# A prologue of an adaptive-norm block on one Trainium2 core: the decay table's round trip put ahead of the bulk loads, and weight checks, casts, a residual, statistics and two flag operations moved

## The chip, the cores and the metric

The kernel runs on one core of one Trainium2 chip (trn2). The metric is the device time of one execution in microseconds (us). The engines are TensorE (PE), VectorE (DVE), ScalarE (ACT), GpSimd (POOL) and SyncE (SP); SP and ACT issue DMAs, and each of the two has one DMA queue in this program.

## The reference

One transformer-like block on x of 4 x 2048 x 256 (float32). A modulation of six rows per batch comes from `silu(c) @ wmod`. With it:

```python
ga = sign(ga) * max(|ga|, 0.25)           # gb likewise
h = layernorm(x) * (1 + ca) + sa
x = x + ga * attn(h)
h = layernorm(x) * (1 + cb) + sb
x = x + gb * ffn(h)
```

`attn` is a linear-attention memory with 4 heads of 64: tokens go in chunks of 64, keys are the normalised `h` of the token before, and each head has a decay `gamma = sigmoid(decay)`. In a chunk the products of keys are weighted by `gamma ** (i - j)`; a unit triangular matrix of 64 x 64 is inverted; then a state of 64 x 64 for each batch and head passes from chunk to chunk. `ffn` has two gated input layers (256 to 1024, silu), two layers 1024 to 1024 with gelu and one back to 256; its weights are -1, 0 or 1 with one scale for each output.

## The kernel before

The 2048 tokens are 32 steps of 64 (`STEPS`). In every step the attention of the step and the dense layers (`l1`, `l2`, `l3`, `y`) of the one before are interleaved on PE. The order on every engine is written out by hand: lists of items such as `("gram", 0)` are walked by each engine's `part()`, which does its own share of that item. `alone` is the list of the first step's attention, with no dense layers to run beside it; `opening` follows it, and ends where the first dense layer (`l1` of the list `second`) can start; then come `second`, `third` and the loop over `mixed`. The engines meet only through semaphores, and each engine works through its items strictly in its list's order, so an item that waits holds back all behind it on that engine. SP and ACT also keep their DMA issues in program order.

What the prologue has to do, and the names:

- **Decay table.** GpSimd computes `powers` (gamma to the distance, L698) from `decay` and the first part of the constants. The table is written to DRAM (`pow_dram`, the DMA `decay_powers<-powers`, semaphore `pow_out`) and read back twice in a shifted form (`hank<-decay_powers`, `pow_in`). PE spreads it (`tables`, L1283), and DVE makes the masks of it (`level_mask` L1047, `intra_mask`). Without them no `near`, `cross` or `far` (products of keys under a mask, on POOL, L617) can be made, so no inverse. DVE copies the turned keys to `rT` behind `level_mask`.
- **Inverse.** `fs` on DVE gives 8 x 8 inverses, `expand` makes `inv`; then `n` 1, 2 and 3 on PE and DVE, then the copies `diag` on ACT (L716), then `solve` (own values and corners).
- **Bulk loads.** SP loads the second part of the modulation weights (`wmod_sb`, 1024 KB), then the dense weights into `w_raw`: 22 loads of 512 KB, two to a unit, 11 units (0 to 10). Unit i is issued only when unit i-3 has landed (`hi_in`). Among them stand the tokens of step 1 (`y<-in_x`) and the key rows of step 0 (`kg<-r`, `last<-r`).
- **Checks.** The item `check` on ACT reads the low halves of a unit of weights (L731, 11 in all, `checked`), to see that they are zero. DVE reduces the result (`flag` 0, L1071, waits for all 11), PE turns it, DVE makes `flag_i` of it (`flag` 1), and PE and SP branch on it; on the given weights the branch to the exact rounded weights is taken.
- **Casts.** The item `round` copies units into `w_hi` (four on POOL, L628, the rest on ACT and POOL later). PE's first `l1` waits for those four, for `intra_ready` and for `xl_ready`.
- **Gates.** `cols` multiplies `wmod_sb` on PE (L1265) and makes the small gate columns on DVE (`gate_done` counts to 5); `spread` and `gates` widen them.
- **Residual and statistics.** `residual` on POOL is `base` = x + h * ga in two operations (L643, L645); `stats` are the layer norm's sums of step 1 on DVE (L838), `length` the reciprocal norm `rinv` on POOL (L605), `unit` the normalised keys `r` on DVE (L878).
- **End of the prologue.** `attn_out` gives x1 of step 0, `norm2` its normalised form `xn` (DVE L1007), `turn` and `ln2` (ACT, eight operations) `h2`, `parts` its two halves `xh` and `xl`, `sweep` 1 and `intra` belong to step 1's attention. `warm` items are matmuls on PE whose result nobody reads (L1158).

## Time and profile before

| | |
|---|---|
| median of 3 runs | 1749.15 us (1746.56 to 1749.63) |
| the profiled execution | 1747.17 us, its span 1745.3 us |
| mean granted TensorE clock | 0.993 |
| PE busy | 1714.9 us, 98% of the span |
| DVE, ACT, POOL busy | 64%, 55%, 34% |
| first dense matmul (L1169) | 68.16 us after the span's start |
| DMA traffic by fortieths of the span | 327 GB/s in the first (43.6 us), 3 to 31 GB/s in every later one |

The table is read from the page: its part 1 gives the busy times, part 2 the granted clock by slices, part 3 the queues. The span is the trace's own length; the time beside it also holds what lies around the span, 1.87 us here. Times of steps below are counted from the span's start.

### The profile page before, as it was taken

How to read it: one execution, taken by the hardware profiler on the slowest of the kernel's cores; microseconds unless marked ns; L12 is line 12 of the kernel's file. 1: busy time of each engine (PE TensorE's matmuls, PEld its weight loads, DVE VectorE, ACT ScalarE, POOL GpSimd, SP SyncE). 2: the span in 40 equal slices, each digit the busy share in tenths (PEclk: the TensorE clock that was granted, in tenths of full speed). 3: DMA queues.
4: the chain of work that ended last, by engine and by line, in shares of the span. 5: the costliest groups of instructions: out<-in, count | busy, mean ns of one | idle time of the engine just before them, and what ended most of it. 6: DMA issues, size and time to landing. Idle time of an engine off the chain costs nothing.

```text
span 1745.3 us, 60527 instructions
## 1 busy us (share of the span) xinstructions
PE 1714.9 (98%) x25489; PEld 1650.2 (95%) x25489; DVE 1115.6 (64%) x3038; ACT 964.3 (55%) x2251; POOL 592.9 (34%) x694
## 2 busy tenths in 40 slices
PE   7799999999999999999999999999999999999999
PEld 4698999999999999999999999999999999999998
DVE  4778666666666666666666676666666666666432
ACT  4664555555555555555555555555555555555554
POOL 3544332342332343333243333243233233343111
PEclk8999999999999999999999999999999999999999
DMA  9001000000000000000000000000000000000000
GB/s 327 31 14 29 15 23 23 15 23 11 24 23 24 18 20 11 24 23 24 18 20 14 22 23 23 18 19 20 15 23 23 22 16 19 16 23 17 8 3 12
DMA packets 37108, 47.08 MB, mean 27 GB/s; under 512 B 8864, under 2 KB 29088, under 8 KB 36832
## 3 DMA queue, kind: packets, MB, share of 16 engines
q1 hardware_dynamic: 35360, 41.80, 8.6%
q8 instruction: 206, 3.38, 0.8%
q10 hardware_dynamic: 1472, 1.34, 0.3%
q14 instruction: 70, 0.57, 0.1%
HBM read 22.53 MB, written 8.39 MB: 18 GB/s over the span
## 4 chain that ended last, share of the span: by engine, by line
PE 94%; DVE 1%; POOL 1%; issue 1%; DMA 1%; ACT 1%; ACTq 0%; SPq 0%; POOLq 0%; DVEq 0%
PE mlp L1169 64%; PE mlp L1241 6%; PE solo L1169 3%; PE solo L1316 3%; PE duo L1445 3%; PE solo L1142 2%; PE duo L1135 1%; PE duo L1366 1%; PE duo L1130 1%; PE duo L1434 1%; PE solo L1454 1%; PE duo L1339 1%; PE solo L1152 1%; PE duo L1330 1%; PE duo L1436 1%
## 5 line engine op out<-in xcount | busy, mean ns | idle before, releaser
L1169 PE MATMUL mlp<-act_hi,w_hi 128*128 128x256 f32 x4096 | 969.5, 283 | 1.2 <-POOL act_lo L664 0.5
L1169 PE MATMUL mlp<-act_lo,w_hi 128*128 128x256 f32 x4096 | 946.8, 278 | 0.0
L1169 PEld LDWEIGHTS mlp<-act_hi,w_hi 128*128 128x128 f32 x4096 | 771.1, 188 | 10.0 <-POOL act_lo L664 1.2
L1169 PEld LDWEIGHTS mlp<-act_lo,w_hi 128*128 128x128 f32 x4096 | 771.9, 188 | 1.0 <-issue 0.2
L806 ACT ACTIVATE full<-mlp,scale_sb 128x256 f32<-128x256 f32 x512 | 246.4, 481 | 558.5 <-PE mlp L1169 558.3
L897 DVE TENSOR_TENSOR act_lo<-full,act_hi 128x256 fp32r<-128x256 f32 x512 | 240.4, 470 | 318.5 <-ACT act_hi L807 315.9
L664 POOL TENSOR_TENSOR act_lo<-full,act_hi 128x256 fp32r<-128x256 f32 x256 | 186.6, 736 | 497.8 <-ACT act_hi L796 497.5
L807 ACT ACTIVATE act_hi<-mlp,scale_sb 128x256 fp32r<-128x256 f32 x512 | 242.6, 474 | 0.0
L1169 PE MATMUL mlp<-xh,w_hi 128*128 128x256 f32 x768 | 189.1, 284 | 4.8 <-issue 2.3
L1169 PE MATMUL mlp<-xl,w_hi 128*128 128x256 f32 x768 | 188.2, 281 | 0.0
L605 POOL TENSOR_TENSOR rstd<-ve,minus_half 128x2 f32<-128x2 f32 x64 | 49.0, 766 | 338.5 <-DVE ve L846 338.3
L1021 DVE SCALAR_TENSOR_TENSOR full<-mlp,scale_sb,gate 128x256 f32<-128x256 f32 x192 | 92.9, 484 | 98.1 <-ACT gate L791 93.0
L791 ACT ACTIVATE gate<-mlp,scale_sb 128x256 f32<-128x256 f32 x192 | 90.9, 474 | 109.5 <-PE mlp L1169 109.4
L1169 PEld LDWEIGHTS mlp<-xh,w_hi 128*128 128x128 f32 x768 | 144.2, 188 | 6.1 <-issue 4.6
L1169 PEld LDWEIGHTS mlp<-xl,w_hi 128*128 128x128 f32 x768 | 144.9, 189 | 0.0
L1241 PE MATMUL mlp<-w_hi,act_hi 128*128 128x256 f32 x512 | 118.2, 277 | 0.0
L1241 PE MATMUL mlp<-w_hi,act_lo 128*128 128x256 f32 x512 | 118.1, 277 | 0.0
L605 POOL TENSOR_TENSOR rinv<-ssm,minus_half 128x8 f32<-128x8 f32 x32 | 52.7, 1647 | 184.4 <-DVE ssm L875 184.4
L796 ACT CAST act_hi<-full 128x256 fp32r<-128x256 f32 x256 | 101.7, 397 | 11.3 <-DVE full L1021 11.3
L1241 PEld LDWEIGHTS mlp<-w_hi,act_hi 128*128 128x128 f32 x512 | 96.1, 188 | 0.1
L1241 PEld LDWEIGHTS mlp<-w_hi,act_lo 128*128 128x128 f32 x512 | 96.2, 188 | 0.0
L780 ACT ACTIVATE h<-solo,sbm,cb 128x64 f32<-128x64 f32 x256 | 84.0, 437 | 2.0 <-PE solo L1454 2.0
(177 smaller groups left out, 2677.4 us busy)
## 6 DMA issues: line engine op xcount, KB each, us to landing
w_raw<-in_wts SPq DMA_DIRECT2D x22, 512.0 KB, 8.4
kg<-r SPq DMA_DIRECT2D x64, 126.0 KB
xin<-in_x SPq DMA_DIRECT2D x62, 128.0 KB
out_y<-y SPq DMA_DIRECT2D x62, 128.0 KB, 2.5
step_and_inv<-square_t SPq DMA_DIRECT2D x56, 64.0 KB, 2.0
wmod_sb<-in_wmod SPq DMA_DIRECT2D x1, 1024.0 KB, 8.2
kg<-last SPq DMA_DIRECT2D x64, 2.0 KB
last<-r SPq DMA_DIRECT2D x64, 2.0 KB, 1.8
```

Source lines behind the costliest of these rows:

```text
L605: pool.tensor_tensor(dst[:], src[:], minus_half[:, 0:src.shape[1]], ALU.pow).then_inc(done, 1)
L664: pool.tensor_tensor(act_lo[0][:, k, :], full[k % 3][:], act_hi[0][:, k, :].bitcast(F32), ALU.subtract).then_inc(l_ready[0], 1)
L780: ins = act.activation(h2[:].rearrange("p k b n -> p (k b n)")[:, cols], solo[1][:, cols], ACT.Identity, bias=sbm[:, k, b:b + 1], scale=cb ...
L791: act.activation(gate[k % 2][:], gated[k % 3][:, 0:TOK], ACT.Silu, scale=scale_sb[:, 0, k:k + 1]).then_inc(l_act[0], 1)
L796: act.copy(act_hi[0][:, j, :], full[j % 3][:]).then_inc(l1_hi, 1)
L806: act.activation(full[k % 2][:], mlp[k % 2][:, 0:TOK], ACT.Gelu, scale=s)
L807: act.activation(act_hi[layer % 2][:, k, :], mlp[k % 2][:, 0:TOK], ACT.Gelu, scale=s).then_inc(l_act[layer], 1)
L897: dve.tensor_tensor(act_lo[layer % 2][:, k, :], full[k % 2][:], act_hi[layer % 2][:, k, :].bitcast(F32), ALU.subtract).then_inc(l_ready[la ...
L1021: dve.scalar_tensor_tensor(full[k % 3][:], up, s, gate[k % 2][:], ALU.mult, ALU.mult).then_inc(prod_ready, 1)
L1169: mm = pe.matmul(dst, *general_ops, start=is_first and i == 0, stop=is_last and i == 1)
L1241: mm = pe.matmul(mlp[k][:, 0:D], *ops, start=j == 0 and i == 0, stop=j == HK - 1 and i == 1)
L1316: mm = pe.matmul(solo[0][:, b * D:(b + 1) * D], hT[:, kt, b, :], wv_sb[:, kt, :], start=kt == 0, stop=kt == KT - 1)
```

## The change

The table's write and read-back go from ACT's queue to SP's and stand ahead of `wmod_sb` and of all weights, which SP issues only after the write is confirmed and the two reads are issued. ACT still waits for `pow_out` before it loads `wr_turned`. The checks stand later in ACT's list (`CHECKS` also groups them otherwise), one `warm` less is asked at `cols` and at the jump, and the first items of DVE's `opening` are in another order. POOL's first casts wait for `gate_done`, its second `gram` waits for `xn2_ready`, and DVE waits for `base` one operation later.

```diff
-CHECKS = {0: (0,), 1: (1, 2), 2: (3,), 3: (4, 5, 6, 7), 4: (8, 9), 5: (10,)}
-WARM_START, WARM_NORM, WARM_COLS, WARM_LINK, WARM_JUMP = 3, 1, 2, 1, 4
+CHECKS = {0: (0,), 1: (1,), 2: (2, 3, 4, 5, 6), 3: (7, 8), 4: (9,), 5: (10,)}
+WARM_START, WARM_NORM, WARM_COLS, WARM_LINK, WARM_JUMP = 3, 1, 1, 1, 3
...
     opening = [(*item, 0) for item in (
-        ("norm2", 0), ("turn", 0), ("flag", 0), ("ln2", 0), ("ln2", 1), ("fs", 0), ("flag", 1), ("warm", WARM_JUMP), ("sweep", 1), ("parts", 0), ("intra", 0), ("u", 0),
+        ("flag", 0), ("norm2", 0), ("turn", 0), ("ln2", 0), ("ln2", 1), ("flag", 1), ("warm", WARM_JUMP), ("fs", 0), ("parts", 0), ("sweep", 1), ("intra", 0), ("u", 0),
...
             load_tokens(0)
             sp.dma_start(con[:, CO_FIRST:CO_N], const[:, CO_FIRST:CO_N]).then_inc(const_in, 16)
+            sp.wait_ge(pow_ready, 1)
+            sp.dma_start(pow_dram, powers[:]).then_inc(pow_out, 16)
+            sp.wait_ge(pow_out, 16)
+            for c in range(2):
+                shifted = bass.AP(pow_dram.tensor, pow_dram.offset, [[H, C], [1, C * H]])
+                sp.dma_start(hank[half(c)].rearrange("p n h -> p (n h)"), shifted).then_inc(pow_in, 16)
             sp.dma_start(wmod_sb[:, :, 2 * D:6 * D], wmod[:, :, 2 * D:6 * D]).then_inc(wmod_in[1], 16)
...
                     if name == "round":
+                        if k == 0:
+                            pool.wait_ge(gate_done, 5)
...
                     if name == "gram":
+                        if items is alone and a == 1:
+                            pool.wait_ge(xn2_ready, 1)
...
-            act.wait_ge(pow_ready, 1)
-            act.dma_start(pow_dram, powers[:]).then_inc(pow_out, 16)
             act.wait_ge(mod_full, 2)
             act.copy(sa[:, 1, :], duo[1][:, 1, 0:D])
             act.activation(ca1[:, 1, :], duo[1][:, 1, D:2 * D], ACT.Identity, bias=1.0).then_inc(shift_ready, 1)
             act.wait_ge(pow_out, 16)
-            for c in range(2):
-                shifted = bass.AP(pow_dram.tensor, pow_dram.offset, [[H, C], [1, C * H]])
-                act.dma_start(hank[half(c)].rearrange("p n h -> p (n h)"), shifted).then_inc(pow_in, 16)
...
                         xo = x1[g]
-                        dve.wait_ge(base_ready, now)
+                        if items is not alone:
+                            dve.wait_ge(base_ready, now)
                         dve.wait_ge(ao_full, now)
                         dve.tensor_tensor(xo[:], duo[1][:, 0, :].rearrange("p (b n) -> p b n", b=NB),
                                           ga, ALU.mult).then_inc(ao_scaled, 1)
+                        if items is alone:
+                            dve.wait_ge(base_ready, now)
```

In `alone` the items move so: `check` 0 from the front to behind `gram`; `check` 1 from ahead of `gram` to behind `cols`, beside `check` 2; `stats` of step 1 from ahead of `n` 2 to behind it; `residual` 0 from behind the state to ahead of `length`; `check` 4 (one unit of the two that were at 4 before) to behind `start_r`.

The first place is SP's program from its fifth row on (`hank` is the table read back, `y` the tokens of step 1). Before:

```order
L573 DMA con<-in_const 128x558
L574 DMA wmod_sb<-in_wmod 128x2x1024
L579 DMA w_raw<-in_wts 128x1024 x4
L582 DMA y<-in_x 64x2x256 x2
L579 DMA w_raw<-in_wts 128x1024 x2
L579 DMA w_raw<-in_wts 128x1024 [waits hi_in0]
```

Now:

```order
L573 DMA con<-in_const 128x558
L575 DMA decay_powers<-powers 128x4 [waits pow_ready]
L579 DMA hank<-decay_powers 64x256 [waits pow_out]
L579 DMA hank<-decay_powers 64x256
L580 DMA wmod_sb<-in_wmod 128x2x1024
L585 DMA w_raw<-in_wts 128x1024 x4
L588 DMA y<-in_x 64x2x256 x2
L585 DMA w_raw<-in_wts 128x1024 x2
L585 DMA w_raw<-in_wts 128x1024 [waits hi_in0]
```

The modulation weights and every weight unit now stand behind a wait for `pow_ready` and one for `pow_out`.

The second place is ACT's program from the copies of step 0's key products (`gram`) to the block-diagonal inverse (`diag`); `low_bits` rows are checks, and hi_in0 to hi_in10 are the eleven units. Before:

```order
L731 ACTIVATE low_bits,slot_low<-w_raw 128x2048 [waits checked,hi_in2]
L762 COPY gram<-duo 128x256 [waits gram_full]
L762 COPY gram<-duo 128x256
L731 ACTIVATE low_bits,slot_low<-w_raw 128x2048 [waits checked,hi_in3]
L757 COPY v<-solo 128x512 [waits v_full]
L731 ACTIVATE low_bits,slot_low<-w_raw 128x2048 [waits checked,hi_in4]
L731 ACTIVATE low_bits,slot_low<-w_raw 128x2048 [waits checked,hi_in5]
L731 ACTIVATE low_bits,slot_low<-w_raw 128x2048 [waits checked,hi_in6]
L731 ACTIVATE low_bits,slot_low<-w_raw 128x2048 [waits checked,hi_in7]
L716 ACTIVATE diag<-duo,con 128x8x32 [waits rest_full]
L716 ACTIVATE diag<-duo,con 128x8x32
L739 COPY gate_cols<-gate_col 128x1024 [waits gate_done]
```

Now:

```order
L772 COPY gram<-duo 128x256 [waits gram_full]
L772 COPY gram<-duo 128x256
L741 ACTIVATE low_bits,slot_low<-w_raw 128x2048 [waits hi_in0]
L767 COPY v<-solo 128x512 [waits v_full]
L741 ACTIVATE low_bits,slot_low<-w_raw 128x2048 [waits checked,hi_in1]
L741 ACTIVATE low_bits,slot_low<-w_raw 128x2048 [waits checked,hi_in2]
L741 ACTIVATE low_bits,slot_low<-w_raw 128x2048 [waits checked,hi_in3]
L741 ACTIVATE low_bits,slot_low<-w_raw 128x2048 [waits checked,hi_in4]
L741 ACTIVATE low_bits,slot_low<-w_raw 128x2048 [waits checked,hi_in5]
L741 ACTIVATE low_bits,slot_low<-w_raw 128x2048 [waits checked,hi_in6]
L726 ACTIVATE diag<-duo,con 128x8x32 [waits rest_full]
L726 ACTIVATE diag<-duo,con 128x8x32
```

The checks of units 0 to 2 have moved behind the copies of `gram`, and ahead of `diag` the last check is now that of unit 6 where it was that of unit 7.

The third place is DVE's program at the end of the prologue, from x1's variance on. Before:

```order
L846 TENSOR_SCALAR ve<-mv 128x2 [waits ln2_mv]
L1007 SCALAR_TENSOR_TENSOR xn<-x_0,mv,rstd 128x256 [waits ln2_rstd]
L1007 SCALAR_TENSOR_TENSOR xn<-x_0,mv,rstd 128x256
L1071 TENSOR_REDUCE any_low<-slot_low 128x1 [waits checked]
L947 TENSOR_REDUCE low<-near 128x64 [waits near_ready]
L948 COPY sub<-con 128x8x7
```

Now:

```order
L851 TENSOR_SCALAR ve<-mv 128x2 [waits ln2_mv]
L1079 TENSOR_REDUCE any_low<-slot_low 128x1 [waits checked]
L1015 SCALAR_TENSOR_TENSOR xn<-x_0,mv,rstd 128x256 [waits ln2_rstd]
L1015 SCALAR_TENSOR_TENSOR xn<-x_0,mv,rstd 128x256
L1082 TENSOR_REDUCE row_low<-duo 1x1 [waits flag_row]
L1084 TENSOR_SCALAR flag_i<-row_low 1x1 [waits flag_col]
```

The reduction of all eleven checks (`any_low`) now stands ahead of `xn`, and the reduction of `near` behind both operations of the flag.

## Rows read from the trace of the kernel before

**Rows 1.** The page's part 2: granted clock by fortieth of the span.

```profile
PEclk8999999999999999999999999999999999999999
```

**Rows 2.** Chain of waits, first 70 us: start, us, what.

```profile
7.78 6.20 DMA decay_powers<-powers
...
14.54 7.71 DMA hank<-decay_powers
...
23.55 1.09 DVE level_mask L1047 x3
...
38.25 1.72 PE duo L1126 x32
...
59.76 1.82 DVE xn L1007 x2
...
66.70 1.45 issue
68.16 2.15 PE mlp L1169 x16
```

**Rows 3.** DMA issues of the first 100 us: count, size of one, median us to landing.

```profile
decay_powers<-powers ACTq DMA_DIRECT2D x1, 2.0 KB, 6.2
```

**Rows 4.** DMA issues of the whole span (the page's part 6).

```profile
step_and_inv<-square_t SPq DMA_DIRECT2D x56, 64.0 KB, 2.0
...
last<-r SPq DMA_DIRECT2D x64, 2.0 KB, 1.8
```

**Rows 5.** Windows: length; PE, PEld, DVE, ACT, POOL busy; clock, DMA share, GB/s.

```profile
12.30:42.50 30.20, 20.64 (x190) 14.72 (x190) 15.50 (x60) 17.42 (x20) 6.29 (x8) 0.72 1.02 349
...
9.50:14.10 4.60, 2.88 (x10) 1.00 (x8) 3.22 (x7) 0.66 (x2) 0.67 (x2) 1.00 1.03 409
...
40.00:80.00 40.00, 31.06 (x483) 23.81 (x483) 31.21 (x87) 26.51 (x53) 24.13 (x26) 1.00 0.19 69
81.00:87.00 6.00, 6.00 (x83) 5.71 (x85) 2.04 (x9) 1.01 (x3) 1.70 (x2) 0.50 0.00 1
```

**Rows 6.** Timeline of DVE, 12 to 55 us.

```profile
16.00 0.69 DVE L878 TENSOR_TENSOR r<-h,rinv 128x512 f32<-128x512 f32 x1 [1.82 <-POOL rinv L605]
...
35.65 0.42 DVE L965 TENSOR_TENSOR inv<-sub,con 128x256 f32<-128x256 f32 x1
...
42.78 1.24 DVE L887 TENSOR_TENSOR square_t<-square_t,con 128x256 f32<-128x256 f32 x1
...
53.75 1.27 DVE L878 TENSOR_TENSOR r<-x,rinv 128x512 f32<-128x512 f32 x1
```

**Rows 7.** Timeline of PE, the spare matmuls before `n` 1 and before the jump.

```profile
34.49 3.76 PE L1158 MATMUL duo<-o_state 128*128 128x512 f32 x4
...
62.28 3.60 PE L1158 MATMUL duo<-o_state 128*128 128x512 f32 x8
```

**Rows 8.** Timeline of POOL, 42 to 56 us.

```profile
42.70 4.22 POOL L628 CAST w_hi<-w_raw 128x1024 fp32r<-128x1024 f32 x4
...
51.59 1.64 POOL L605 TENSOR_TENSOR rinv<-ssm,minus_half 128x8 f32<-128x8 f32 x1 [4.67 <-DVE ssm L875]
...
54.55 1.60 POOL L645 TENSOR_TENSOR base<-xin,base 128x512 f32<-128x512 f32 x1
```

**Rows 9.** Timeline of ACT, 38 to 60 us.

```profile
38.97 1.91 ACT L731 ACTIVATE low_bits<-w_raw 128x2048 f32<-128x2048 uint16 x1 [1.90 <-DMA w_raw<-in_wts]
...
44.91 0.84 ACT L716 ACTIVATE diag<-duo,con 128x256 f32<-128x256 f32 x2 [3.93 <-PE duo L1366]
...
49.03 1.07 ACT L744 COPY mods<-mlp 128x512 f32<-128x512 f32 x2
...
55.93 0.58 ACT L754 COPY rT<-mlp 128x512 f32<-128x512 f32 x1
...
57.36 0.65 ACT L762 COPY gram<-mlp 128x256 f32<-128x256 f32 x2 [0.85 <-PE mlp L1330]
57.89 1.92 ACT L731 ACTIVATE low_bits<-w_raw 128x2048 f32<-128x2048 uint16 x1
```

More of the change, by code:

```diff
@@ L310, in main @@
     alone = [(*item, 0) if len(item) == 2 else item for item in (
-        ("check", 0), ("warm", WARM_NORM), ("start", 0), ("warm", WARM_NORM), ("tables", 0), ("start_r", 0), ("masks", 0), ("ready", 0), ("check", 1), ("gram", 0),
-        ("heads", 0), ("check", 2), ("values", 0), ("cols", 0), ("warm", WARM_COLS), ("check", 3), ("intra", 0), ("fs", 0), ("fs", 1), ("fs", 2), ("fs", 3), ("expand", 0), ("far", 0),
-        ("heads", 1), ("n", 1), ("stats", 0, 1), ("warm", WARM_LINK), ("n", 2), ("cols", 1), ("warm", WARM_LINK), ("n", 3), ("spread", 0),
-        ("round", 0), ("round", 1), ("warm", WARM_LINK), ("norm", 0, 1), ("keys", 0), ("wr", 0), ("square", 0, 1), ("length", 0, 1),
-        ("solve", 0), ("gates", 0), ("solve", 1), ("start", 0, 1), ("check", 4), ("residual", 0), ("state", 0), ("unit", 0, 1), ("attn_out", 0),
-        ("start_r", 0, 1), ("gram", 1, 1), ("check", 5), ("values", 0, 1), ("pred", 0, 1))]
+        ("warm", WARM_NORM), ("start", 0), ("warm", WARM_NORM), ("tables", 0), ("start_r", 0), ("masks", 0), ("ready", 0), ("gram", 0),
+        ("check", 0), ("heads", 0), ("values", 0), ("cols", 0), ("warm", WARM_COLS), ("check", 1), ("check", 2), ("intra", 0), ("fs", 0), ("fs", 1), ("fs", 2), ("fs", 3), ("expand", 0), ("far", 0),
+        ("heads", 1), ("n", 1), ("warm", WARM_LINK), ("n", 2), ("stats", 0, 1), ("cols", 1), ("warm", WARM_LINK), ("n", 3), ("spread", 0),
+        ("round", 0), ("round", 1), ("warm", WARM_LINK), ("norm", 0, 1), ("keys", 0), ("wr", 0), ("square", 0, 1), ("residual", 0), ("length", 0, 1),
+        ("solve", 0), ("gates", 0), ("solve", 1), ("start", 0, 1), ("check", 3), ("state", 0), ("unit", 0, 1), ("attn_out", 0),
+        ("start_r", 0, 1), ("check", 4), ("gram", 1, 1), ("check", 5), ("values", 0, 1), ("pred", 0, 1))]
     opening = [(*item, 0) for item in (
-        ("norm2", 0), ("turn", 0), ("flag", 0), ("ln2", 0), ("ln2", 1), ("fs", 0), ("flag", 1), ("warm", WARM_JUMP), ("sweep", 1), ("parts", 0), ("intra", 0), ("u", 0),
+        ("flag", 0), ("norm2", 0), ("turn", 0), ("ln2", 0), ("ln2", 1), ("flag", 1), ("warm", WARM_JUMP), ("fs", 0), ("parts", 0), ("sweep", 1), ("intra", 0), ("u", 0),
         ("residual", 0), ("rg", 0), ("round", 2), ("silu", 0))]
```

## The prediction

> **What bounds the kernel now.** I read the page's clock row first, then the chain of waits, then the timelines of the first 70 us. From the second fortieth on the granted clock shows 9 tenths or more throughout [rows 1], and PE is busy 98% of the span: behind the prologue there is nothing for this change to win, since it touches only lists that run before the first dense matmul. The chain of waits shows the prologue as a series of single dependencies, and it ends with the first L1169 at 68.16 us [rows 2]. Whatever moves this start moves the end by as much, unless the granted clock behaves otherwise afterwards. So I work out when the first L1169 starts.
>
> The longest stretch in the chain is the table's round trip: `powers` is ready at 7.78, the write takes 6.20 us, a read 7.71, and the masks can be made at 23.55 only [rows 2, 3]. The same kinds of DMA take 1.8 us (2 KB) and 2.0 us (64 KB) later in the kernel [rows 4], and the bulk loads run beside the round trip at 409 GB/s with all engines busy [rows 5]. So some 10 us of it are queueing.
>
> **Round trip and masks.** Now SP issues nothing large before the write. What is in flight at 7.8 is the tail of the early loads. I take the later prices: 7.8 + 1.8 for the write, 1.2 for the issue of two reads (0.6 each, as between the end of the write, 13.98, and the start of the read, 14.54 [rows 2]), 2.0 for landing: 12.8. By the prices of before it would be 7.8 + 6.2 + 1.2 + 7.7 = 22.9. I take the low end, since the row of 6.2 us lies under traffic that is no longer there. Up to 16.7 it costs nothing: DVE finishes the keys `r` of step 0 at 16.0 + 0.69 = 16.69 [rows 6], and stands ahead of `level_mask` in its list. The masks then start at 16.7 instead of 23.55: 6.9 us earlier. The turning of `r` (PE) runs beside them as before.
>
> **Inverse.** `inv` was made at 35.65, so now at 28.8. Before, `n` 1 did not start on it but at 38.25, at the end of four spare matmul passes that began at 34.49 (two `warm`, 1.88 each at the clock of 1.2 GHz) [rows 2, 6, 7]. One of them is gone: PE is free at 38.25 - 6.9 - 1.9 = 29.5, just after `inv` with its 0.42. Then `square_t` took 1.24 us with POOL's casts beginning at 42.70 beside it [rows 6, 8]; its neighbours of the same shape take 0.42 (`inv`). The casts now wait for `gate_done`, which comes later than `square_t`: 0.8 saved. `stats` of step 1 moves behind `n` 2 and fills DVE's time under `n` 3, where it was under `n` 2: nothing. The copies `diag` could so start at 44.91 - 6.9 - 1.9 - 0.8 = 35.3 [rows 9].
>
> **The new wait: weights ahead of `diag`.** ACT now has the check of unit 6 in front of `diag`, with those of 2 to 5, and all weights are issued late: SP gets to `wmod_sb` at about 11 and the stream flows from about 12.3, where it flowed from about 5. Up to unit 6 there pass two reads (0.13 MB), `wmod_sb` 1.05, seven units 7.34, `y` 0.26 and, on ACT's queue, `wr_turned` 0.26: 9.0 MB. At the 349 GB/s of the whole stream that takes 25.9 us, at the 409 of its undisturbed part 22.1 [rows 5]: unit 6 is in at 34.4 to 38.2. A check is 1.91 and 0.19 for its sum, 2.1. `diag` then starts at 36.5 to 40.3; I take 38.5, nearer to the measured mean with less beside the stream than before (the reads no longer cut into it). So 3.2 of the 9.6 us are given back here, 6.4 remain. The older checks fit: ACT is free from the copies of `gram` (about 20.6), and seven checks and the copy of `v` are 15.3 us, so they alone end no earlier than 35.9.
>
> **From `diag` to `xn`.** Own values, corners, state and output follow `diag` as before, 6.4 earlier. POOL's casts (4.22) start with `gate_done` near 38 to 39.5 and end near 43, before the widened gates are there (49.03 + 1.07 - 6.4 = 43.7, the copies `mods` as they follow `diag` [rows 9]); they delay nothing. POOL then does `residual` first and `rinv` behind it: 43.8, two operations of about 1.3 (1.60 in [rows 8] for the second), `rinv` 1.64, end at 48.2 instead of 53.23. That is 5.0 earlier, 1.4 worse than the rest; but DVE's `r` beside a busy POOL was 1.27 and is 0.69 alone [rows 6, 8], so keys are ready 5.7 to 6.2 earlier, `rT` (55.93 + 0.58) ends at 50.4 [rows 9]. Then ACT: check 2.1, copies of `gram` 0.65, check 2.1: 55.3 [rows 9]. `any_low` on DVE waits for this last check and now stands ahead of `xn`, which could start at 52.7 without it. `xn` so starts at 55.5, where it was 59.76 [rows 2]: 4.3 earlier, and is done in 0.9 instead of 1.82, since POOL's `near` waits for it and no longer runs beside: 5.2 earlier at its end. Unit 10 must be in by 53.2: 13.5 MB from 12.3 are in at 45.3 to 51.0.
>
> **To the first L1169.** `ln2` and `parts` keep their 5.2. `sweep` 1 (three short operations; I put 0.75) now stands between `parts` and `intra`: `intra` ended at 66.70, so 66.70 - 5.2 + 0.75 = 62.3. Before, L1169 did not start at 66.70 but 1.45 later [rows 2], and 2.28 after the end of the spare matmuls (62.28 + 3.60 [rows 7]), which I read as the branch and the fetch of its target. Now PE turns `xn` until 57.1 and has three spare matmuls of 0.9: 59.8, and with 2.28 for the jump 62.1. Both are near 62.3. Sum: 68.16 - 62.3 = 5.9 us earlier, from 6.9 + 1.9 + 0.8 - 3.2 (`diag`), - 1.2 (order of POOL and the flag's wait, net of the faster `xn`), + 0.7 (the jump no longer alone at the end). The profiled execution had 1747.17 with a span of 1745.3, and lies 2.0 below the median 1749.15 of runs that differ by 3.1 us. So 1741.3 for its like, and 1743.3 for the median. I forecast 1743.
>
> **Weighed against the skill.** The Trainium skill, "DMA: Bandwidth & Descriptors", section "Rules for kernel authors", advises to issue a DMA early and to wait on it late; this change issues 12 MB of weights some 7 us later. By that rule the whole delay would show, and the start would be at about 75 instead of 62. In this trace the loads are late enough to be waited for only at one check of 1.90 us [rows 9], so I see it as the rival below and not as the forecast.
>
> **Rivals.** (a) *The stream sets less* (chance 0.17): unit 6 in at 34.4 and PE's clock full earlier, because the long idle before the tables is gone. `diag` at 36.5: 2 us more, and 1 more if the dip of [rows 5] (81 to 87 us at 0.50, the first dense layers at half speed) falls away, half of 6 us at most, 3. Gain 7.5 to 10.5: 1738.5 to 1741.5. For it: 409 GB/s was reached; against: 349 was the mean.
>
> (b) *The clock takes part of it back* (0.25): PE now stands still while ACT works off its checks before `diag`, again before `xn` and again at the jump. Before, with shorter gaps, it had 1.00 from 40 to 80 and then a dip of some 6 us at 0.50, in which L1169 took twice as long [rows 5]. One more such dip costs up to 3 us. Gain 1 to 3.5: 1745.5 to 1748. The Trainium skill, "TensorE: Matmul & The Clock Gate", section "HAM oscillation", says the same of idle gaps; no row here shows what a gap of this size does.
>
> (c) *The round trip stays slow* (0.08): the time is not the traffic's. With 6.2 and 7.7 the masks are where they were, the weights flow from 16.5 on, and unit 10 lands at 49.5 to 55.2. `rT` is then where it was (56.5), the last check ends at 61.4, `xn` starts at 61.6 instead of 59.76, ends at 62.5 (61.58 before), and L1169 starts at 68.2: no change, within 1 us. Against it: 1.8 and 2.0 in 64 and 56 cases [rows 4].
>
> (d) *The end of the weights decides* (0.05), on the other side: everything behind `any_low` waits for unit 10. It is in time up to 53.2; at 59.1 the gain is gone, and at 62.6 the kernel is 3.5 us slower (1752.7, up to 1755). For that the stream would have to run at 13.5 MB in 50.3 us, 268 GB/s throughout, where the mean is 349.
>
> **Numbers.** The forecast (gain 4 to 7.5: 1741.5 to 1745) has 0.45. (a), (b), (c), (d) have 0.17, 0.25, 0.08, 0.05. The range leaves out the far end of (a), half of (c) and (d): 1739.5 to 1748.5. A change under 0.2% (3.5 us) can't be told from none, as the runs before differ by 3.1. Faster: the forecast and (a), and a fifth of (b): 0.67. Within: the rest of (b) and (c): 0.28. Slower: 0.05.
>
> **What would show it.** Right: `decay_powers` lands in about 2 us and `hank` by 13; `level_mask` at 16.7; `n` 1 at 29.5; ACT idle on `w_raw` just before `diag`, `diag` at 36.5 to 40.3; no L628 before 38; `any_low` waiting on ACT's check, at about 55.4; L1169 at 62 to 63. Wrong: `hank` after 17; `diag` after 41; a window of 0.50 clock in the dense layers longer than the 6 us of before; `any_low` waiting for a check that itself waits for DMA.

## The result, and the profile after

The changed kernel is slower, where a gain was forecast. Its median was 1756.42 us (1750.47 to 1758.18) beside 1749.63 us (1746.56 to 1752.77) of the kernel before on the same chip: a ratio of 1.0035 (95% interval 1.0019 to 1.0051). A second measurement beside the last experiments gave 1752.59 against 1750.06 us, 1.0013 (1.0001 to 1.0025). Both say slower, the first by 0.35 and the second by 0.13%. In the last experiments one run of the kernel before (1887.41 us) and one of c2 (4611.85 us, which its median of 12 still holds) were in a slower state, and the ratios leave them out.

The page of the changed kernel, its part 2 (granted clock by fortieths of the span, 43.9 us each):

```profile
PEclk8799999999999999999999999999999999999999
```

Against [rows 1] one digit has changed: the second fortieth (43.9 to 87.8 us) has a clock of 7 tenths, where it had 9. That is the first thing to follow. The chain of waits of the changed kernel, first 80 us (start, us, what):

```profile
16.76 1.00 DVE level_mask L1055 x3
...
28.90 1.92 PE duo L1134 x32
...
37.20 6.96 issue
44.16 1.97 PE solo L1150 x32
...
54.36 0.70 DVE o_state L992
...
58.23 2.00 ACT low_bits L741 x2
...
62.70 0.16 DVE any_low L1079
62.87 0.80 DVE xn L1015 x2
...
68.46 1.26 DVE sub_term L965
69.78 1.19 issue
70.97 0.75 DVE intra L942 x2
71.81 3.76 PE mlp L1177 x16
```

Beside [rows 2]: the masks start at 16.76 instead of 23.55 and `n` 1 at 28.90 instead of 38.25, so by 29 us the kernel is 9.3 us ahead. The first dense matmul (L1177, L1169 before) comes at 71.81 instead of 68.16, 3.65 us behind. So 13 us are lost between `n` 1 and the dense layers, and the stretch of 6.96 us in which PE stands still is the largest piece. The same marks, forecast beside measured (`diag`, `o_state` and `xn` of before by their timelines):

| start, us | before | forecast | after | second profile of after |
|---|---|---|---|---|
| `level_mask` | 23.55 | 16.7 | 16.68 | 17.26 |
| `n` 1 | 38.25 | 29.5 | 28.90 | 30.25 |
| `diag` | 44.91 | 38.5 | 43.14 | 41.45 |
| `o_state` (end of the state's products) | 52.54 | 46.1 | 54.36 | 52.97 |
| `xn` | 59.76 | 55.5 | 62.78 | 63.60 |
| first dense matmul | 68.16 | 62.3 | 71.81 | 72.46 |

What stands ahead of `diag` is in the timeline of ACT (the bracket is the idle time ahead of the row, and what ended it):

```profile
29.86 1.91 ACT L741 ACTIVATE low_bits<-w_raw 128x2048 f32<-128x2048 uint16 x1 [2.81 <-DMA w_raw<-in_wts]
...
37.46 1.91 ACT L741 ACTIVATE low_bits<-w_raw 128x2048 f32<-128x2048 uint16 x1 [0.51 <-DMA w_raw<-in_wts]
...
41.23 1.91 ACT L741 ACTIVATE low_bits<-w_raw 128x2048 f32<-128x2048 uint16 x1 [1.76 <-DMA w_raw<-in_wts]
...
43.14 0.82 ACT L726 ACTIVATE diag<-duo,con 128x256 f32<-128x256 f32 x2
```

Every check from unit 0 on starts when its unit lands, and that of unit 6, the last in front of `diag`, at 41.23. `diag` had its operands from 36.14 on (`n` 3 on PE, 35.40 + 0.74), so ACT's checks hold it back by 7 us, and PE with it.

What PE's clock did, in windows of the changed kernel (length; PE, PEld, DVE, ACT, POOL busy; clock, DMA share, GB/s). The first is the stream up to unit 6, the second PE's pause, the third and the last two are stretches at 0.50:

```profile
12.30:41.20 28.90, 18.45 (x254) 12.55 (x254) 20.70 (x76) 13.72 (x16) 9.80 (x11) 0.87 1.02 344
37.20:44.16 6.96, 0.00 (x1) 0.03 (x1) 6.43 (x11) 4.94 (x7) 4.84 (x5) 0.72 1.01 345
40.30:53.90 13.60, 9.73 (x160) 8.87 (x164) 4.99 (x8) 7.67 (x12) 5.81 (x6) 0.50 0.73 283
...
71.00:77.80 6.80, 5.99 (x28) 6.02 (x29) 2.87 (x10) 1.73 (x5) 1.83 (x2) 0.50 0.00 1
88.00:91.40 3.40, 3.40 (x24) 3.18 (x27) 1.70 (x7) 0.03 (x1) 1.34 (x2) 0.50 0.01 2
```

In [rows 5] the kernel before has 1.00 from 40 to 80 us. Here PE stands still from 37.20, its clock is at 0.50 (1.2 of 2.4 GHz) from 40.3, and it stays there through all that follows `diag`: own values, corners, gate spreading and the state's products. The rows of PE:

```profile
44.16 1.97 PE L1150 MATMUL solo<-v,diag 64*64 64x64 f32 x32 [6.96 <-issue]
45.90 1.89 PE L1143 MATMUL duo<-diag,far 64*64 64x32 f32 x32
47.72 1.97 PE L1280 MATMUL mlp<-con,gate_cols 128*128 128x128 f32 x8
49.61 1.92 PE L1160 MATMUL solo<-vn,mi 32*32 32x64 f32 x32
```

The same four rows took 1.15, 1.10, 1.06 and 1.08 us before. From `diag` to `o_state` it is 11.22 us against 7.63, so a `diag` that is 1.8 us earlier than before becomes an `o_state` that is 1.8 later.

One caution on spans. The profiled executions have 1756.4 us here and 1745.3 before, 11.1 apart, of which the first dense matmul explains 3.65. A second profile of the unchanged kernel (below) has 1753.0, with its first dense matmul at 68.91, only 0.75 later. Behind the prologue two executions of one kernel thus differ by some 7 us, and of the 6.8 us between the two medians above the marks explain about 4. I therefore read mechanisms from the marks up to the first dense matmul, and the size of an effect from the medians.

### The profile page after: what moved, and what is told of

Same layout as the page of the kernel before. It is cut to its first block, busy times and chain, and to the rows that moved or that the text cites. A ratio compares the mean times of both kernels' runs of the same rounds, so it can differ in the third digit from the quotient of the medians.

```text
span 1756.4 us, 60521 instructions
## 1 busy us (share of the span) xinstructions
PE 1720.2 (98%) x25485; PEld 1655.2 (94%) x25485; DVE 1116.8 (64%) x3038; ACT 964.5 (55%) x2251; POOL 592.4 (34%) x694
## 4 chain that ended last, share of the span: by engine, by line
PE 95%; DVE 2%; issue 1%; ACT 1%; POOL 1%; DVEq 0%; ACTq 0%; POOLq 0%
PE mlp L1177 64%; PE mlp L1249 6%; PE solo L1177 3%; PE duo L1453 3%; PE solo L1324 3%; PE solo L1150 2%; PE duo L1143 1%; PE duo L1374 1%; PE duo L1442 1%; PE duo L1138 1%; PE solo L1160 1%; PE solo L1462 1%; PE duo L1347 1%; PE duo L1444 1%; PE duo L1338 1%
## 5 line engine op out<-in xcount | busy, mean ns | idle before, releaser
L1177 PE MATMUL mlp<-act_hi,w_hi 128*128 128x256 f32 x4096 | 971.4, 283 | 1.1 <-POOL act_lo L674 0.6
L1177 PE MATMUL mlp<-act_lo,w_hi 128*128 128x256 f32 x4096 | 948.7, 278 | 0.0
L1177 PEld LDWEIGHTS mlp<-act_hi,w_hi 128*128 128x128 f32 x4096 | 771.1, 188 | 9.8 <-POOL act_lo L674 1.2
L1177 PEld LDWEIGHTS mlp<-act_lo,w_hi 128*128 128x128 f32 x4096 | 771.5, 188 | 1.0 <-issue 0.3
L1177 PE MATMUL mlp<-xh,w_hi 128*128 128x256 f32 x768 | 190.8, 286 | 5.8 <-DVE intra L942 3.1
L1177 PE MATMUL mlp<-xl,w_hi 128*128 128x256 f32 x768 | 189.8, 281 | 0.0
L1177 PEld LDWEIGHTS mlp<-xh,w_hi 128*128 128x128 f32 x768 | 145.5, 189 | 7.0 <-issue 5.5
L1177 PEld LDWEIGHTS mlp<-xl,w_hi 128*128 128x128 f32 x768 | 146.3, 190 | 0.0
```

Source lines behind the costliest of these rows:

```text
L1177: mm = pe.matmul(dst, *general_ops, start=is_first and i == 0, stop=is_last and i == 1)
```

## The experiments

All are timed beside the kernel before. The table has the first dense matmul of each profile, how much earlier (-) or later the second output store is than in the profile of before (195.4 us; it also holds the clock of the first dense layers), and the measured ratio.

| kernel | first dense | second store | ratio (95%) | median, us |
|---|---|---|---|---|
| before | 68.16 | 0 | | |
| before again | 68.91 | +0.2 | 1.0005 (0.9994 to 1.0015) | 1750.41 |
| after | 71.81 | +4.2 | 1.0035 (1.0019 to 1.0051) | 1756.42 |
| after again | 72.46 | +4.9 | 1.0013 (1.0001 to 1.0025) | 1752.59 |
| e1, lists only | 74.68 | +5.9 | 1.0050 (1.0037 to 1.0063) | 1757.64 |
| e2, queue only | 67.93 | -0.8 | 1.0007 (0.9998 to 1.0017) | 1750.59 |
| e3, checks behind `diag` | 67.25 | -0.5 | 1.0015 (1.0006 to 1.0023) | 1751.47 |
| e4, lists only, statistics and casts back | 68.63 | +0.4 | 1.0033 (1.0021 to 1.0046) | 1752.90 |
| e5, opening as before | 68.52 | +0.8 | 1.0010 (0.9998 to 1.0023) | 1749.98 |
| e6, PE kept busy | 67.21 | -0.2 | 1.0014 (1.0004 to 1.0024) | 1749.76 |
| c1, first mend | 67.73 | -1.2 | 1.0006 (0.9996 to 1.0016) | 1749.26 |
| e7, c1 with casts later | 62.77 | -6.0 | 0.9980 (0.9970 to 0.9990) | 1745.91 |
| c2, e7 with another opening | 63.25 | -6.5 | 0.9975 (0.9964 to 0.9986) | 1744.92 |
| e8, PE busy and that opening | 62.17 | -9.4 | 0.9979 (0.9971 to 0.9988) | 1745.82 |

In the first two rows of the second column the measurement's own grain is seen: the kernel before gives 68.16 and 68.91. The ratio of a kernel whose start is where it was lies between 1.0005 and 1.0015 in most runs (e4 is higher). The changed kernel's own second measurement, 1.0013, lies among them, so single remedies are told apart by their marks here, not by their ratios; on the fast side only e7, c2 and e8 stand clear of the kernel before.

**e1: the lists alone.** The changed kernel with the table's DMAs back on ACT's queue and the weights issued at once:

```diff
-            sp.wait_ge(pow_ready, 1)
-            sp.dma_start(pow_dram, powers[:]).then_inc(pow_out, 16)
-            sp.wait_ge(pow_out, 16)
...
+            act.wait_ge(pow_ready, 1)
+            act.dma_start(pow_dram, powers[:]).then_inc(pow_out, 16)
...
```

> The changed kernel with the table's write and read-back put back on ACT's queue and the weights issued at once; all lists, spare matmuls and waits as changed. Theory S (the late weight stream costs: ACT's check of unit 6 ahead of diag, PE's clock after it, last_in): diag starts at 42 to 43, no half-speed stretch between 40 and 54 us, first dense matmul at 66.5 to 68, time within 2 us of the kernel before (1749.6). Theory L (the lists cost: the flag ahead of xn, sweep 1 ahead of intra, residual ahead of rinv): first dense matmul at 70 or later and 3 or more us slower than before.

Measured: 1.0050, the slowest of all, the first dense matmul 6.5 us later than before. The masks are where they were (23.45 us) and `diag` at 44.18 (44.91 before), so the loss comes behind `diag`. The timeline of e1, POOL's casts and the rows of DVE that lie beside them:

```profile
45.91 4.75 POOL L630 CAST w_hi<-w_raw 128x1024 fp32r<-128x1024 f32 x4 [0.63 <-DVE gate_col L1106]
...
47.45 2.31 DVE L870 SCALAR_TENSOR_TENSOR x<-x,rstd,mods 128x256 f32<-128x256 f32 x2
49.68 1.52 DVE L934 TENSOR_TENSOR kg<-kg,tail_decay 128x512 f32<-128x512 f32 x1
50.63 1.71 POOL L645 TENSOR_TENSOR base<-h,mods 128x512 f32<-128x512 f32 x1
51.13 2.71 DVE L918 TENSOR_SCALAR wr_turned<-wr_turned,gam 128x256 f32<-128x256 f32 x2
53.75 0.68 DVE L875 TENSOR_TENSOR r<-x 128x512 f32<-128x512 f32 x1
```

The later casts (45.91 instead of 42.70) fall on the norm and the keys of step 1, and the residual moved forward falls on `wr_turned`. Alone (e7 below) these rows take 0.88, 0.68 and 0.61. DVE reaches the square of the keys at 53.75 where it was at 49.90. So theory L has its number, but by a way that it did not name: most of the loss is made on DVE before `xn`, and the prediction had put it down at nothing. Not every operation of DVE grows beside POOL: the reduction `ss` keeps its 0.69 us beside `base` in e7 (41.45), and `v<-v,duo`, with one of its two inputs in PSUM, keeps 0.68 in the kernel before (66.61).

**e2: the queue alone.** The kernel before with only the round trip moved to SP's queue, ahead of the bulk loads.

```diff
+            sp.wait_ge(pow_ready, 1)
+            sp.dma_start(pow_dram, powers[:]).then_inc(pow_out, 16)
+            sp.wait_ge(pow_out, 16)
...
             sp.dma_start(wmod_sb[:, :, 2 * D:6 * D], wmod[:, :, 2 * D:6 * D]).then_inc(wmod_in[1], 16)
...
```

> The kernel before with only the table's write and read-back moved to SP ahead of the modulation weights and the dense weights. Theory S: the masks come at 16.7 but ACT's check of unit 2 stands ahead of the copies of gram and waits for the stream until about 30, so the inverse chain starts some 4 to 5 us later than before, and the whole is 4 to 8 us slower than before, about as slow as the changed kernel or slower. Theory L: as fast as before or up to 6 us faster, since the lists that cost are not in it.

Measured: 1.0007, no difference, where theory S had 4 to 8 us; `n` 1 comes at 37.36, 0.9 earlier than before and not later. The masks are ready as in the changed kernel (16.41 us), but the copies of `gram` come no earlier. ACT's timeline of e2:

```profile
25.91 1.91 ACT L737 ACTIVATE low_bits<-w_raw 128x2048 f32<-128x2048 uint16 x1 [1.77 <-DMA w_raw<-in_wts]
...
27.82 0.62 ACT L768 COPY gram<-duo 128x256 f32<-128x256 f32 x2
```

A check of a unit that is now late stands in front. So the list of checks had to move with the queue; the one without the other gains nothing, and what was moved too far in e1 loses.

**e3: fewer checks ahead of `diag`.** The changed kernel with

```diff
-CHECKS = {0: (0,), 1: (1,), 2: (2, 3, 4, 5, 6), 3: (7, 8), 4: (9,), 5: (10,)}
+CHECKS = {0: (0,), 1: (1,), 2: (2, 3, 4), 3: (5, 6, 7, 8), 4: (9,), 5: (10,)}
```

> The changed kernel with the checks of units 5 and 6 moved from ahead of diag to the next place for checks (ahead of state). Theory S in its first form (the wait of ACT ahead of diag is what costs): diag at 36 to 37 instead of 43.1, clock 1.00 from 34 to 54 us, first dense matmul at 67 to 68 (now held by last_in at 46.8 and by the checks behind it), 4 us or more faster than the changed kernel. Theory L: the time stays at 1756 within 2 us.

Measured: `diag` at 36.97, right behind `n` 3, 6.2 us earlier than in the changed kernel; own values at 1.15 us; the first dense matmul at 67.25, 4.6 earlier than after. The wait at `diag` is gone, and own values and corners have the full clock. But of the 8 us that `diag` is ahead of before, less than one is left at the end. Timelines of e3, PE and DVE:

```profile
38.02 1.15 PE L1150 MATMUL solo<-v,diag 64*64 64x64 f32 x32
...
48.90 0.77 PE L1453 MATMUL duo<-wr_turned,o_state 128*128 128x256 f32 x1 [2.97 <-DVE o_state L992]
...
46.55 0.68 DVE L876 TENSOR_TENSOR r<-x 128x512 f32<-128x512 f32 x1
47.27 0.69 DVE L878 TENSOR_REDUCE ss<-r 128x8 f32<-128x512 f32 x1
...
48.07 0.68 DVE L992 COPY o_state<-duo 128x512 f32<-128x512 f32 x1
```

PE waits for DVE, and DVE is without a gap from 38.55 on through the lengthened rows of e1: the second loss was hidden behind the first in the changed kernel. Behind this pause of 2.97 us the clock goes to half again: the eight matmuls of L1453 take 3.57 us for 1.97 before, at a mean clock of 0.55 from 48.5 to 51. In the time little of the gain can be seen: 1751.47 us is 5.0 us under the changed kernel's first median and 1.1 under its second.

**e4: e1 with its causes taken out.** Statistics of step 1 back ahead of `n` 2, casts without their wait for the gates:

```diff
-                        if k == 0:
-                            pool.wait_ge(gate_done, 5)
...
```

> The kernel of the run with the lists alone (weights at once, 1757.6 us), and the statistics of step 1 put back ahead of n 2, the casts' wait for gate_done taken out. In that run POOL's four casts ran from 45.9 to 50.7 beside DVE's normalisation, keys and wr (8.0 us for what took 2.8 before), so keys were squared at 53.75 instead of 49.90. Theory P (GpSimd's large operations, put beside DVE's large ones, cost): casts start 2 to 3 us earlier, squaring at 49.5 to 51.5, 2 to 4 us faster, 1753.5 to 1755.5. Rival F (only the flag's and sweep's places cost): squaring stays near 53.7 and the time within 1.5 us of 1757.6.

Measured: first dense matmul at 68.63 instead of 74.68, 6 us; median 1752.90 against 1757.64 (ratios 1.0033 and 1.0050, from two measurements). The casts start at 40.54 and are done at 44.74; the norm's rows behind them take 0.88 each, `kg` 0.68, `wr_turned` 0.61, the square is at 48.01. The square is 5.7 us earlier than in e1, and all behind it 4 to 6: this is what the lists cost up to the first dense matmul. Statistics and casts were put back together, so their shares are not told apart, and the 1.0033 of this kernel is more than its marks explain (see Open).

**e5: the opening as before.** The flag behind `xn`, `sweep` 1 ahead of `parts`.

```diff
-        ("flag", 0), ("norm2", 0), ("turn", 0), ("ln2", 0), ("ln2", 1), ("flag", 1), ("warm", WARM_JUMP), ("fs", 0), ("parts", 0), ("sweep", 1), ("intra", 0), ("u", 0),
+        ("norm2", 0), ("turn", 0), ("flag", 0), ("ln2", 0), ("ln2", 1), ("fs", 0), ("flag", 1), ("warm", WARM_JUMP), ("sweep", 1), ("parts", 0), ("intra", 0), ("u", 0),
```

> The changed kernel with the list opening as before (xn ahead of the flag's reduction, fs ahead of flag 1, sweep 1 ahead of parts). Theory P: xn starts near 61 instead of 62.8 but ln2 on ACT still waits for the last check (62.6), so that saves under 1.5 us; sweep 1, which took 2.8 us beside POOL's base where 0.75 was priced, no longer stands between parts and intra, which saves 2; first dense matmul at 69 to 70 (71.8), 1753.5 to 1754.5 if the clock behaves as in the changed kernel. Rival S (the stream alone costs): within 1 us of 1756.4.

Measured: 68.52 against 71.81. `xn` follows its factor at once (59.81), and `intra` is done at 66.78. What is left is the jump. Not all of the 3.3 us is the opening's: unit 6 landed earlier here than in the changed kernel's first profile, with `diag` at 40.10 and the last check done at 61.97 instead of 62.58. From the end of the last check to the first dense matmul it is 6.55 us here, and 9.23 and 9.07 in the two profiles of the changed kernel, so the opening is worth about 2.6. The timelines of e5, DVE and PE:

```profile
63.92 0.14 DVE L1084 TENSOR_SCALAR flag_i<-row_low 1x1 int32<-1x1 f32 x1
...
62.43 2.74 PE L1166 MATMUL duo<-o_state 128*128 128x512 f32 x6
68.52 0.55 PE L1177 MATMUL mlp<-xh,w_hi 128*128 128x256 f32 x1 [3.35 <-issue]
```

The matmul comes 4.46 us after the flag is written (64.06), and 3.35 after six spare matmuls; in the kernel before it came 4.83 after the flag (63.33) and 2.28 after eight. The distance to the flag is the steady one: 4.4 to 5.0 us in both profiles of before and in e2, c1, e7, c2 and e8. In the changed kernel (flag at 64.02) the jump alone would have allowed 68.4 to 69.0; `intra`, done at 71.72, was later.

**e6: PE kept busy.** The changed kernel with six more spare matmul passes in PE's pause:

```diff
-        ("round", 0), ("round", 1), ("warm", WARM_LINK), ("norm", 0, 1)
+        ("round", 0), ("round", 1), ("warm", 7), ("norm", 0, 1)
```

> The changed kernel with six more spare matmuls on PE between n 3 and the own values, where PE stood still from 37.2 to 44.2 us and then had half the clock until 53.9. Theory C (the clock takes back what the earlier diag gave): clock 1.00 from 34 to 54, own values to state 3 to 4 us shorter, output state at 50.5 to 51.5 instead of 54.4; the keys' square stays at 46.8 (it waits for last<-r), so the normalised keys come at 51.5 to 53 instead of 55.6; 2 to 4 us faster, 1752.5 to 1754.5. Rival: the spare matmuls run past 44.2 or the checks on ACT hold all behind them; no change within 1 us.

Measured: PE's timeline and the window of e6:

```profile
37.45 6.28 PE L1166 MATMUL duo<-o_state 128*128 128x512 f32 x14
43.65 1.15 PE L1150 MATMUL solo<-v,diag 64*64 64x64 f32 x32
...
34.00:60.00 26.00, 22.00 (x407) 15.26 (x407) 16.59 (x44) 19.15 (x28) 11.01 (x11) 0.98 0.66 230
```

The same window has a clock of 0.74 in the changed kernel and 0.66 in its second profile. From own values to `o_state` it is 6.19 us against 10.20 and 10.41 (6.59 before). So 4 us of the loss are the clock, and the clock fell because PE stood still. The Trainium skill, "TensorE: Matmul & The Clock Gate", section "HAM oscillation", says that a long enough wait of PE puts its clock back to half; the trace agrees, with 0.98 against 0.74 in the same window. The first dense matmul is at 67.21 instead of 71.81; of these 4.6 us some belong to `diag`, at 41.04 here because unit 6 landed earlier. The median says less: 1.0014, where the changed kernel had 1.0035 and 1.0013.

**c1: a first mend,** of e3's kind (`CHECKS` 2: (2, 3, 4), 3: (5, 6, 7), 4: (8, 9)), the opening of before, and the key rows issued two units earlier on SP.

> A mended version: the table's round trip first as in the change, ACT's checks of units 5 and 6 behind diag (one place for 5 to 7, one for 8 and 9), opening as before, key rows of step 0 copied two units earlier on SP. If stream, opening and last_in are the three costs: diag at 36 to 37, square of keys at 42 to 44 instead of 46.8, xl at 62 to 63, intra right behind at 63.5 to 64, first dense matmul at 65 to 66 where the kernel before has 68.2: 1745 to 1748, 2 to 4 us faster than before. If ACT's checks alone hold the end of the prologue, first dense matmul at 67 to 68 and no difference from before.

Measured: 67.73, ratio 1.0006, not the 65 to 66 that three costs should have given. The row `last<-r` now comes in time, yet the square of the keys is at 47.12 instead of 46.82: DVE's `wr_turned` beside the residual takes 2.70 there instead of 0.60 in the changed kernel, since in that one DVE came to it before the residual. So the wait for that DMA was not the only limit: without it the lengthened rows hold the square as long.

**e7: the casts out of DVE's way.** c1, with the two items `round` on POOL behind `attn_out` instead of ahead of `norm` 1.

```diff
-        ("round", 0), ("round", 1), ("warm", WARM_LINK), ("norm", 0, 1)
+        ("warm", WARM_LINK), ("norm", 0, 1)
...
-        ("unit", 0, 1), ("attn_out", 0),
+        ("unit", 0, 1), ("attn_out", 0), ("round", 0), ("round", 1),
```

> The first mended version (1749.3 us), with POOL's four casts moved from beside DVE's normalisation, keys and wr to behind the reciprocal root of x1. Theory P (an operation of DVE takes about twice as long beside a large one of POOL): the normalisation takes 0.88 an operation instead of 1.65 and 2.31 for two, keys 0.68 instead of 1.52, wr 0.61 instead of 2.70 for two; the square of the keys starts at 42 to 43.5 instead of 47.1, and PE does not stand still from 46.4 to 49.5. End of the prologue still held by ACT's checks: last check ends at 59 to 60 instead of 61.2; 1 to 3 us faster, 1746.5 to 1748.5. Rival: the DVE operations stay slow without the casts beside them, or the casts double xn and hold the first dense matmul; no change or slower.

Measured: 0.9980, the first dense matmul at 62.77, 5.0 us earlier than c1. Timelines of e7, DVE and POOL:

```profile
38.67 0.88 DVE L871 SCALAR_TENSOR_TENSOR x<-x,rstd,mods 128x256 f32<-128x256 f32 x2
39.47 0.68 DVE L935 TENSOR_TENSOR kg<-kg,tail_decay 128x512 f32<-128x512 f32 x1
40.07 0.61 DVE L919 TENSOR_SCALAR wr_turned<-wr_turned,gam 128x256 f32<-128x256 f32 x2
40.73 0.69 DVE L876 TENSOR_TENSOR r<-x 128x512 f32<-128x512 f32 x1
...
49.90 2.42 DVE L1015 SCALAR_TENSOR_TENSOR xn<-x,mv,rstd 128x256 f32<-128x256 f32 x2 [0.81 <-POOL rstd L611]
...
49.82 4.37 POOL L636 CAST w_hi<-w_raw 128x1024 fp32r<-128x1024 f32 x4
```

The square is 6.4 us earlier than in c1. The weights still stream beside these rows (363 GB/s from 37.2 to 44.2), so it was not the DMA traffic that lengthened them. The casts now lie beside `xn` and make that 2.42 instead of 0.88, which costs nothing since the end of the last check (55.88) is later than what follows it.

**c2 and e8.** Both take an opening in which the flag stands behind `xn` and its two operations ahead of `fs` and `sweep` 1; c2 is e7 with it, e8 is the changed kernel with it and with PE kept busy (`("warm", 5)` at e6's place), its checks and casts left where the change put them.

```diff
+        ("norm2", 0), ("turn", 0), ("flag", 0), ("ln2", 0), ("ln2", 1), ("flag", 1), ("warm", 4), ("fs", 0), ("sweep", 1), ("parts", 0), ("intra", 0), ("u", 0),
```

> The same with the flag's second operation ahead of fs (before it stood behind it), sweep 1 ahead of parts, and four spare matmuls before the jump. In all profiles so far the first dense matmul came 4.4 to 4.8 us after flag_i was written, or right behind intra where that was later. Theory J (the jump runs from flag_i): flag_i 1.5 us earlier, first dense matmul at 64 to 65.5 where before has 68.2 and the first mended version 67.7, no half-speed stretch at it: 1744 to 1746.5. Rival (the jump runs from the last spare matmul): 66 to 67.

> The changed kernel with two small mends together: four more spare matmuls on PE ahead of the own values (six more gave 1749.8), and the opening with xn ahead of the flag, sweep 1 ahead of parts, four spare matmuls before the jump (the opening alone gave 1750.0). If clock and opening are separate costs of about 6 and 3 us, both together give the first dense matmul at 64.5 to 66 and 1744.5 to 1747; if each only removes the same half-speed stretch at the first dense layers, 1749 to 1750 as each alone.

Measured: 0.9975 and 0.9979, 1744.92 and 1745.82 us, which can't be told apart; both are faster than before, and their first dense matmuls (63.25 and 62.17) came earlier than either expectation had them. Windows of e8:

```profile
34.00:60.00 26.00, 22.87 (x376) 15.21 (x369) 19.33 (x52) 22.21 (x37) 13.08 (x13) 0.97 0.66 228
60.00:92.00 32.00, 28.43 (x515) 26.07 (x514) 22.55 (x60) 22.08 (x44) 19.70 (x21) 1.00 0.01 3
```

Here the first dense layers have a clock of 1.00, where the changed kernel has 0.79 and the kernel before 0.89 in 60 to 92 us; so the second store is 9.4 us earlier, 3.4 more than the first dense matmul. That is what the prediction's rival (a) had priced at up to 3. Only some 4 of the 9.4 are left in the median, and where the rest goes is not settled (below). In c2 the matmul starts 4.93 us after the flag (58.32), and the flag waits for the last check: that is the path that is left. The other opening brought nothing over e7 there: the flag is at 58.32 where e7 has it at 57.81.

**Before and after again.** The unchanged kernel, and the changed one, once more.

> The kernel before, unchanged, as a second profile of it and as a measure of what no change looks like. If the growth of the distance inside the loop (from 4.2 us at the second output to 11.0 at the last, in the first pair of profiles) is chance, this profile differs from the first one of before in the loop by some us too, with the prologue the same within 1 us; if it belongs to the changed kernel, the two profiles of before keep within 1.5 us of each other to the end.

> The changed kernel once more, unchanged: a second profile of it and its time in the same call as the three below. If half speed after the idle PE and at the first dense layers belongs to the change and not to one execution, this profile shows both again, and the first dense matmul at 71 to 72 us; the time at 1755 to 1758 where the kernel before has 1748 to 1750.

Measured: 1.0005 for the unchanged kernel, with the second profile's span 7.7 us longer than the first; it lags the first by 0.2 us at the second store and by 8.2 near the end, growing in steps of up to 1.3 us from one store to the next. So a growing distance in the loop also comes without any change. The changed kernel has unit 6 at 39.55 instead of 41.23 in its second profile, `diag` at 41.45, the clock at 0.66 in 34 to 60 us, and the same end: 72.46.

## Why the prediction was wrong

Three terms of the sum failed. The bytes ahead of unit 6 were counted too low, and `diag` came 4.6 us later than forecast. The clock behind `diag` was put at nothing and cost 3.6. `sweep` 1 in front of `intra` took 2.0 more than priced. With the first alone the start would have been 66.9, still 1.3 us before the 68.16 of the kernel before; it is the clock that turned the gain into a loss.

**The round trip: right.** `decay_powers` took 1.4 us, forecast 1.8 by the later rows; the masks start at 16.68 (forecast 16.7), `n` 1 at 28.90 (29.5). Of the 6.2 and 7.7 us of before most was time in a queue, as read from [rows 3, 4]. e2 has the same masks from this move alone. The issues of the first 80 us of the changed kernel:

```profile
hank<-decay_powers SPq DMA_DIRECT2D x2, 64.0 KB, 4.4
...
decay_powers<-powers SPq DMA_DIRECT2D x1, 2.0 KB, 1.4
```

The read was not right: it took 4.4 us where 2.0 was taken, and PE could start on the table at 14.65. That cost nothing, since DVE came to the masks no earlier than 16.68 in any case. And no run parts the traffic from the queue: the table left the bulk loads' way and ACT's queue in one step.

**The new wait at `diag`: the mechanism right, its size wrong.** It was forecast at 36.5 to 40.3 us and was 43.14 (41.45 in the second profile). The rate was well chosen: 344 GB/s up to 41.2, beside 349. The bytes were not. By 41.20 the DMAs had moved 28.9 us x 344 GB/s = 9.9 MB, where I counted 9.0 up to unit 6, as if a unit were in when all ahead of it and itself had passed. SP has up to three units under way, so parts of units 7 and 8 move beside unit 6, and the key rows of step 0 with them. 9.9 MB at 349 from 12.3 on give 40.8. This term was 4.6 us short (3.0 in the second profile), and e3 shows that the checks of units 5 and 6 in front of `diag` are all of the wait. The rule of the Trainium skill that was weighed there ("DMA: Bandwidth & Descriptors", "Rules for kernel authors", issue early and wait late) is borne out in its second half: with the same late issue and a later wait, `diag` is 6.2 us earlier.

**The clock behind it: the step that turned the gain into a loss.** "Own values, corners, state and output follow `diag` as before" took durations from a trace in which PE had 1.00 there. PE's pause was in the forecast (rival (b)), but it was priced as one more dip in the dense layers, "up to 3 us", and given 0.25. It came at once instead, in small dependent matmuls: 10.2 us for 6.6 (3.6 lost), and again for 10.2 us in the dense layers (6.8 before). e6 shows it: with PE busy the stretch took 6.19 us. The forecast itself contained the pause, since it moved `n` 3 to 35.4 and `diag` to 38.5; a row for what such a pause does was missing, and "no row here shows it" should have widened the range upward past no change.

**DVE beside POOL: costed at nothing, and wrong.** The prediction asked only whether the casts delay POOL's own next work ("they delay nothing"), and took 0.8 us as saved because `square_t` was clear of them. They moved onto the norm and keys of step 1, on the same path: 1.65, 2.31 and 1.52 us for rows of 0.88, 0.88 and 0.68. The row that could have told it was in [rows 6]: `square_t` 1.24 beside them, where `inv` of the same shape took 0.42, and I used it for the gain alone. In the changed kernel this loss is covered, since the square then waits for `last<-r` until 46.82 and `o_state` comes at 54.36 only. e1 and e3 uncover it and add `wr_turned` beside the residual (2.71 for 0.61); e4 and e7 remove it.

**From `xn` on.** `any_low` ahead of `xn` behaved as foreseen: `xn`'s factor was there at 60.80, and it started at 62.78 behind the last check. Of `sweep` 1, priced 0.75, the trace shows this (DVE, then POOL):

```profile
68.46 1.25 DVE L965 TENSOR_TENSOR sub_term<-sub_row,low 128x64 f32<-128x64 f32 x1
69.74 1.30 DVE L967 TENSOR_TENSOR sub<-sub,sub_term 128x64 f32<-128x64 f32 x1
...
68.36 1.27 POOL L651 TENSOR_TENSOR base<-x,mods 128x512 f32<-128x512 f32 x1 [1.84 <-DVE xl L1023]
69.70 1.26 POOL L653 TENSOR_TENSOR base<-y,base 128x512 f32<-128x512 f32 x1
```

The operations take 0.23 us elsewhere and here each ends with one of POOL's two operations of `base` (1.27 and 1.26), which `parts` releases; so moving `sweep` behind `parts` put it under that: 2.77 us from 68.20 to 70.97, 2.0 more than priced. My reading of the jump ("2.28 after the end of the spare matmuls") was wrong too; it hangs on the flag, 4.4 to 5.0 us after it (e5). It made no difference here, since `intra` was later.

**The sum.** Forecast 62.3, measured 71.81: 4.6 (`diag`), 3.6 (clock), 2.2 (from `xn` to the first dense matmul, 2.0 of it `sweep`), less 1.0, since between `o_state` and `xn` less stood in the way than forecast: 9.4 of the 9.5. These are distances between marks, so they must add up; that the causes are these is shown by e3 (the wait), e6 (the clock) and e5 (the opening). On the rivals: (b) had the cause with too small a price, (c) is excluded by the masks, (d) did not happen (the last two checks started at 58.23 and 60.67 without a wait for DMA), and (a)'s clock gain is real in e8, though unit 6 was late, not early, in both profiles of the changed kernel.

**Open.** The loop behind the prologue differs by up to 8 us between executions of one kernel, so a gain of 9.4 us at the second store (e8) shows as about 4 in the median, and e4, whose marks are those of before, has 1.0033. The five other kernels that start within 1 us of the kernel before (e2, e3, e5, e6, c1) all have ratios above 1, from 1.0006 to 1.0015, so a small cost behind the prologue that they share is possible and not shown. No run here separates what sets it.

## What to carry over

A wait that leaves PE idle is paid a second time in PE's clock: price what follows it at the half clock, or fill the gap with matmuls that nobody reads. Before moving a large operation on GpSimd, list what VectorE does beside its new place, not what it frees at the old one. When a transfer is made late, move the instructions that wait for it behind everything that doesn't need it, and count the bytes under way beside it, not only those ahead of it.

## What the runs showed of the hardware

- VectorE beside a large GpSimd operation: pairs of operations that take 0.88 us took 1.65 and 2.31, one of 0.68 took 1.52, a pair of 0.61 took 2.70, and operations of 0.23 us took as long as the GpSimd operation itself (1.25 and 1.30 beside 1.27 and 1.26). A reduction (0.69, e7) and an operation with one input in PSUM (0.68, kernel before) kept their time beside `base`.
- After PE had stood still from 37.20 us the granted clock was 0.50 from 40.3 to 53.9; 32 matmuls of 64x64 took 1.97 us for 1.15.
- From the write of a flag by VectorE to the first matmul behind the branch on it: 4.4 to 5.0 us in the eight profiles in which nothing later held it.
- A 2 KB write to DRAM took 1.4 us on SP's queue with nothing large under way, and 6.2 on ACT's queue beside the bulk loads; which of the two differences counts is not separated.
